# Mamba in four segments of 512 columns, with the projections of one segment beside the scans of another

## The reference

```python
def _mamba(x, in_w, conv_w, conv_b, xproj_w, dt_w, dt_b, A_log, D, out_w):
    xz = jnp.einsum('bld,ed->ble', x, in_w)
    xi, z = jnp.split(xz, 2, axis=-1)               # 512 channels each
    xi = jax.nn.silu(_dw_conv(xi, conv_w, conv_b))   # 4 taps along the tokens
    xdb = jnp.einsum('bld,ed->ble', xi, xproj_w)     # 128 + 16 + 16 rows
    dtr, Bm, Cm = (xdb[..., :DTR], xdb[..., DTR:DTR + DS], xdb[..., DTR + DS:])
    dt = jax.nn.softplus(jnp.einsum('blr,dr->bld', dtr, dt_w) + dt_b)
    y = _selective_scan(xi, dt, Bm, Cm, -jnp.exp(A_log), D)
    y = y * jax.nn.silu(z)
    return jnp.einsum('bld,ed->ble', y, out_w)
# scan, for each of 16 states: h = exp(dt * A) * h + (dt * x) * B;  y += h * C;  then y += x * D
h = gelu(img_patches @ w_in.T + b_in)
r = _mamba(h, fm...) + flip(_mamba(flip(h, 1), bm...), 1) + h
```

## Time and profile before

| | |
|---|---|
| median of 3 runs | 1244.85 us (1243.49 to 1244.88) |
| profiled execution | 1242.37 us, span of its trace 1240.3 us, mean granted TensorE clock 0.906 |
| lead-in of the Mamba, to the first scan | 543.0 to 625.0 us |
| scan, forward | 625.0 to 834.5 us |
| between the scans | 834.5 to 916.4 us |
| scan, backward | 916.4 to 1123.5 us |
| after the last product | 1123.5 to 1141.5 us |

### The profile page before, as it was taken

The page is one execution under the profiler, slowest core; times in us unless marked ns, Lnnn a source line. Parts: engine busy times, 40 slices in busy tenths (PEclk is TensorE's granted clock), DMA queues, the critical chain, the costliest instruction groups (busy, mean ns, idle before and its releaser), DMA issues. The chain is left out here.

```text
span 1240.3 us, 11914 instructions
## 1 busy us (share of the span) xinstructions
PE 990.9 (80%) x3880; PEld 620.1 (50%) x3880; DVE 914.3 (74%) x872; ACT 494.2 (40%) x804; POOL 689.1 (56%) x325
## 2 busy tenths in 40 slices
PE   6889858999999999959657676779947677668498
PEld 3566646888888888735312222226312222223376
DVE  4577746777777777755598999895399899994732
ACT  2666522434443344335733334343543333332231
POOL 1355522566655666500279999970069999991100
PEclk9899968999999999979877999889968888988799
DMA  3000024343244324120225444540314443530001
GB/s 102 1 1 0 1 85 138 105 132 118 89 118 119 122 85 118 47 72 1 106 102 167 138 169 170 168 141 1 106 35 168 169 168 138 173 132 0 1 1 34
DMA packets 42050, 115.92 MB, mean 93 GB/s; under 512 B 8752, under 2 KB 13872, under 8 KB 41888
## 3 DMA queue, kind: packets, MB, share of 16 engines
q1 hardware_dynamic: 42016, 115.50, 28.8%
HBM read 113.98 MB, written 1.51 MB: 93 GB/s over the span
## 5 line engine op out<-in xcount | busy, mean ns | idle before, releaser
L1143 POOL TENSOR_TENSOR uB<-u,Bb 128x1024 f32<-128x1024 f32 x128 | 304.1, 2398 | 34.2 <-DMA Cb<-bc_rows 13.6
L1224 PE MATMUL m_ps<-hV,ident 128*128 128x512 f32 x336 | 206.2, 750 | 129.0 <-DVE hV L1204 129.0
L768 POOL TENSOR_TENSOR lutw<-lutw,lt 128x860 f32<-128x860 f32 x80 | 200.1, 2501 | 149.0 <-DVE lt L745 143.3
L1199 DVE TENSOR_TENSOR_SCAN m_ps<-m_ps,uB 128x1024 f32<-128x1024 f32 x84 | 191.9, 2284 | 16.2 <-POOL uB L1143 15.7
L1224 PEld LDWEIGHTS m_ps<-hV,ident 128*128 128x128 f32 x336 | 67.8, 223 | 259.2 <-DVE hV L1204 205.9
L1166 ACT ACTIVATE m_ps<-zero 128x4 f32<-128x4 f32 x128 | 22.6, 177 | 269.2 <-DVE hV L1204 222.3
L1204 DVE TENSOR_TENSOR hV<-m_ps,Cb 128x1024 f32<-128x1024 f32 x84 | 102.9, 1225 | 9.0 <-DVE m_ps L1199 0.9
L1150 POOL TENSOR_TENSOR hP<-hS,Cb 128x1024 f32<-128x1024 f32 x44 | 103.8, 2358 | 6.2 <-DVE hS L1195 6.2
L1195 DVE TENSOR_TENSOR_SCAN hS<-m_ps,uB 128x1024 f32<-128x1024 f32 x44 | 100.3, 2280 | 1.1 <-POOL uB L1143 1.1
L1224 PE MATMUL m_ps<-hP,ident 128*128 128x512 f32 x176 | 90.5, 640 | 0.6 <-POOL hP L1150 0.6
L385 POOL TENSOR_TENSOR prob<-prob,ri 128x1024 f32<-128x1024 f32 x32 | 60.6, 1895 | 53.1 <-DVE ri L463 53.1
(11 more groups left out here) (223 smaller groups left out, 2035.3 us busy)
## 6 DMA issues: line engine op xcount, KB each, us to landing
Bb<-bc_rows SPq DMA_DIRECT2D x64, 512.0 KB, 3.5
Cb<-bc_rows SPq DMA_DIRECT2D x64, 512.0 KB, 4.9
wr<-in_moe_w SPq DMA_DIRECT2D x41, 384.0 KB, 4.2
cwb<-cw_rows SPq DMA_DIRECT2D x16, 512.0 KB, 4.0
cwb<-cw_rows SPq DMA_DIRECT2D x16, 384.0 KB, 4.5
cwb<-cw_rows SPq DMA_DIRECT2D x16, 256.0 KB, 3.8
lut_f<-in_lut_idx SPq DMA_DIRECT2D x1, 2144.0 KB, 8.7
cwb<-cw_rows SPq DMA_DIRECT2D x16, 128.0 KB, 3.9
```

Source lines behind the costliest of these rows:

```text
L768: e.tensor_tensor(part, part, lt[:, q, :], ALU.add).then_inc(s_la, 1)
L1143: e.tensor_tensor(uB[:, n % UBUF, :], u[:, d, :], Bb[:, q, :], ALU.mult).then_inc(s_ub, 1)
L1199: e.tensor_tensor_scan(a[:, way], a[:, way], uB[:, n % UBUF, way], 0.0, ALU.mult, ALU.add).then_inc(s_sc, 1)
L1224: mm = e.matmul(ya[n % 2][:, h * HALF:(h + 1) * HALF], g.ident[:, :], at[:, h * HALF:(h + 1) * HALF], start=False, stop=False, skip_group_ ...
```

## The change

The two directions are cut into four segments: seg 0 and 1 are the forward direction over the first and the second two sequences, seg 2 and 3 the backward one. One block holds all of it. A step now works on 512 columns (HALF), so there are 256 steps (STEPS), 64 for each segment (SSTEP) and 32 for each pair of channel blocks (PSTEP). `on_pool`, LATE and the numbers of uB, hV and hP buffers are as before; da has three banks instead of two. A row of B and of C is 256 KB each.

Only the projection of segment 0 stands ahead of the scans. Each engine has a `Side` program for each segment, a generator that names the step at which its next piece is due; after the engine's own work of a step, `advance` runs the pieces that are due. During segment s it does the projection of segment s + 1 (x and convolution in steps 2 to 26, B, C and low rank from 34, dt from 43), the gate's z of that segment, and the output projection of segment s - 1. What is left at the end of a segment is run by `finish`.

The convolution is four float32 matmuls with diagonal matrices for each channel block on PE; POOL makes the 16 diagonals (`tensor_scalar` of the unit matrix) of a direction, those of the backward direction in steps 36 to 51 of segment 0. ACT copies its result from PSUM and adds the bias; Silu of x and of z are one operation of 128 x 2048 each. Softplus keeps dt in PSUM (ln, addition and product with x), and ACT copies it to SBUF. The product hV of step n is now made after the scan of step n + 1. The store of B and C is issued by ACT. SP loads the backward direction's input weights after row 22 and those of x-projection and dt after row 32; ACT and DVE split the former at the end of segment 1. Eight PSUM banks: two sums ya, three da, three side banks.

```diff
+NSEG = 4
+NHS = HALF // SEQ
+PSTEP = 2 * DS
+SSTEP = 2 * PSTEP
+STEPS = NSEG * SSTEP
+ROWS = 3
+UBUF, CBUF, PBUF, DABUF = 3, 3, 2, 3
+LATE = 2
+GATE_AT = 2
...
+class Side:
+    def __init__(self, program):
+        self.program, self.due = program, -1
+    def advance(self, step):
+        while self.due <= step:
+            self.due = next(self.program, NEVER)
+    def finish(self):
+        self.advance(NEVER - 1)
...
+def place(n):
+    pair = n // PSTEP
+    return n // SSTEP, pair, 2 * (pair % 2) + n % 2, n % 2, n // 2, n // 2 % ROWS
...
+        ya = [c.ps(ctx, f"ya{i}", [P, HALF]) for i in range(2)]
+        da = [c.ps(ctx, f"da{i}", [P, HALF]) for i in range(DABUF)]
+        S0, S1, S2 = (c.ps(ctx, f"side{i}", [P, HALF]) for i in range(3))
+        DTB = [S2, S0, S1, S2]
...
+        def x_tensor(e, k, m):
+            if m:
+                e.wait_ge(s_raw, DB * k + m)
+            elif k:
+                e.wait_ge(s_u, DB * (k - 1) + 2)
+                e.wait_ge(s_dtc, DB * (k - 1) + 2)
+                e.wait_ge(s_zc, DB * k - 1)
+            yield from in_rows(e, k, m, S0, s_x)
+        def conv_tensor(e, k, m):
+            e.wait_ge(s_raw, DB * k + m + 1)
+            if m:
+                e.wait_ge(s_cv, DB * k + m)
+            elif k:
+                e.wait_ge(s_u, DB * (k - 1) + 3)
+                e.wait_ge(s_dtc, DB * (k - 1) + 3)
+                e.wait_ge(s_zc, DB * k)
+            for t in range(DCONV):
+                if t:
+                    yield
+                o = t if k < 2 else 2 * PADC - t
+                mm = e.matmul(S1[:, :], sc.dg[:, m, t, :], raw[:, m % 2, :, o:o + SEQ], start=t == 0,
+                              stop=t == DCONV - 1)
+            mm.then_inc(s_c, 1)
...
+            step = 2
+            for work in (x_tensor(e, k, 0), x_tensor(e, k, 1), conv_tensor(e, k, 0), x_tensor(e, k, 2),
+                         conv_tensor(e, k, 1), x_tensor(e, k, 3), conv_tensor(e, k, 2), conv_tensor(e, k, 3)):
+                for _ in work:
+                    step += 1
+                    yield step
+                step += 1
+                yield step
...
+        def side_tensor(e, seg):
+            if seg == NSEG - 1:
+                yield 26
+                yield from out_tensor(e, seg - 1, 26)
+                return
+            k = seg + 1
+            yield 2
+            yield from project_tensor(e, k)
+            yield 26
+            if k == 1:
+                yield from gate_tensor(e, k, [26, 28, 30, 32])
+            else:
+                yield from out_tensor(e, k - 2, 26)
+            yield 34
+            yield from rows_tensor(e, k)
+            yield 43
+            dt_tensor(e, k, 0)
+            yield 44
+            dt_tensor(e, k, 1)
+            yield 45
+            dt_tensor(e, k, 2)
+            yield 50
+            dt_tensor(e, k, 3)
+            if k > 1:
+                yield 51
+                yield from gate_tensor(e, k, [51, 54, 56, 58])
...
+        def exp_abs(e, k, d):
+            e.wait_ge(s_dm, DB * k + d + 1)
+            e.activation(e1[:, d % 2, :], DTB[d][:, :], ACT.Abs, bias=ws[k // 2].dtb[:, d:d + 1]).then_inc(s_ab, 1)
+            e.wait_ge(s_ab, DB * k + d + 1)
+            e.activation(e1[:, d % 2, :], e1[:, d % 2, :], ACT.Exp, scale=-1.0).then_inc(s_e1, 1)
+        def log(e, k, d):
+            e.wait_ge(s_mx, DB * k + d + 1)
+            e.wait_ge(s_e1, DB * k + d + 1)
+            e.activation(DTB[d][:, :], e1[:, d % 2, :], ACT.Ln, bias=1.0).then_inc(s_ln, 1)
+        def keep_dt(e, k, d):
+            e.wait_ge(s_u, DB * k + d + 1)
+            e.activation(dt[:, k % 2, d, :], DTB[d][:, :], ACT.Copy).then_inc(s_dtc, 1)
...
+        def side_scalar(e, seg):
+            if seg < NSEG - 1:
+                yield from project_scalar(e, seg + 1)
+            if seg == 0:
+                yield 32
+                copy_z(e, 1, 0)
+                yield 33
+                copy_z(e, 1, 1)
+            else:
+                yield 31
+                silu_z(e, seg)
+            if seg < NSEG - 1:
+                silu_x(e, seg + 1)
+            e.preload_act_table_set("natural_log_exp_and_others")
...
+        def softplus(e, k, d):
+            e.wait_ge(s_ln, DB * k + d + 1)
+            e.wait_ge(s_mx, DB * k + d + 1)
+            e.tensor_tensor(DTB[d][:, :], DTB[d][:, :], u[:, k % 2, d, :], ALU.add).then_inc(s_dt, 1)
+            e.wait_ge(s_dt, DB * k + d + 1)
+            e.tensor_tensor(u[:, k % 2, d, :], DTB[d][:, :], xi[:, k % 2, d, :], ALU.mult).then_inc(s_u, 1)
...
+                for r in range(STEPS // 2):
+                    q, s, seg = r % ROWS, r % DS, r // (SSTEP // 2)
+                    if r % (SSTEP // 2) == 0:
+                        e.wait_ge(s_bc, 16 * (seg + 1))
+                    if r >= ROWS:
+                        done = 2 * (r - ROWS) + 2
+                        e.wait_ge(s_ub, done)
+                        e.wait_ge(s_hv, vector_steps(done))
+                        e.wait_ge(s_hp, pool_steps(done))
+                    for i in range(2):
+                        e.dma_start(BC[:, q, i, :], dram["bc"][i * DS + s:i * DS + s + 1, half_of(seg)]
+                                    .broadcast_to([P, HALF])).then_inc(s_row[q], 16)
+                    if r == SSTEP // 2 - 10:
+                        e.wait_ge(s_z, 2 * DB)
+                        in_weights(c, dram, "bm", sc)
+                    if r == SSTEP // 2:
+                        e.wait_ge(s_dm, 2 * DB)
+                        e.wait_ge(s_xl, 2)
+                        dt_weights(c, dram, "bm", sc)
...
+                for n in range(STEPS + LATE):
+                    if n < STEPS:
+                        seg, pair, d, b, r, q = place(n)
+                        if n % PSTEP < 2:
+                            e.wait_ge(s_u, DB * seg + d + 1)
+                        if b == 0:
+                            e.wait_ge(s_row[q], 32 * (r // ROWS + 1))
+                        if n >= UBUF:
+                            e.wait_ge(s_sc, n - UBUF + 1)
+                        e.tensor_tensor(uB[:, n % UBUF, :], u[:, seg % 2, d, :], BC[:, q, 0, :],
+                                        ALU.mult).then_inc(s_ub, 1)
+                    m = n - LATE
+                    if m >= 0 and on_pool(m):
+                        k, q = pool_steps(m), place(m)[5]
+                        e.wait_ge(s_sc, m + 1)
+                        if k >= PBUF:
+                            e.wait_ge(s_ap, k - PBUF + 1)
+                        e.tensor_tensor(hP[:, k % PBUF, :], hS[:, k % 2, :], BC[:, q, 1, :],
+                                        ALU.mult).then_inc(s_hp, 1)
+                    side.advance(n)
...
+                def product(n):
+                    k, q = vector_steps(n), place(n)[5]
+                    if k >= CBUF:
+                        e.wait_ge(s_av, k - CBUF + 1)
+                    e.wait_ge(s_sc, n + 1)
+                    e.tensor_tensor(hV[:, k % CBUF, :], da[n % DABUF][:, :], BC[:, q, 1, :], ALU.mult).then_inc(s_hv, 1)
...
+                    e.wait_ge(s_da, 2 * n + 2)
+                    e.wait_ge(s_ub, n + 1)
+                    way = slice(None) if seg < 2 else slice(None, None, -1)
+                    a = da[n % DABUF]
+                    if on_pool(n):
+                        k = pool_steps(n)
+                        if k >= 2:
+                            e.wait_ge(s_hp, k - 1)
+                        e.tensor_tensor_scan(hS[:, k % 2, way], a[:, way], uB[:, n % UBUF, way], 0.0,
+                                             ALU.mult, ALU.add).then_inc(s_sc, 1)
+                    else:
+                        e.tensor_tensor_scan(a[:, way], a[:, way], uB[:, n % UBUF, way], 0.0,
+                                             ALU.mult, ALU.add).then_inc(s_sc, 1)
+                    if n and not on_pool(n - 1):
+                        product(n - 1)
+                    side.advance(n % SSTEP)
...
+                def add(n, at, done):
+                    return e.matmul(ya[n % 2][:, :], g.ident[:, :], at, start=False, stop=False,
+                                    skip_group_check=True).then_inc(done, 1)
```

More of the change, by code:

```diff
@@ L853, in split_weights @@
-def split_weights(c, name, sc):
-    s_wh, s_wl = c.sem(name + "_wh"), c.sem(name + "_wl")
-    parts = [slice(i * D, (i + 1) * D) for i in range(2 * DI // D)]
-    def high(e, w):
-        e.wait_ge(w.ready, w.count)
-        for p in parts:
-            e.activation(sc.wh[:, :, p], w.win[:, :, p], ACT.Copy).then_inc(s_wh, 1)
-    def low(e, w):
-        for i, p in enumerate(parts):
-            e.wait_ge(s_wh, i + 1)
-            e.tensor_tensor(sc.wl[:, :, p], w.win[:, :, p], sc.wh[:, :, p].bitcast(F32),
-                            ALU.subtract).then_inc(s_wl, 1)
-    return high, low
+NSEG = 4
@@ new lines, with on_pool @@
+NHS = HALF // SEQ
[6 more added lines that the diff above has]
+GATE_AT = 2
+NEVER = 10 ** 6
```

(52 more changed lines are left out.)

762 lines of the change are left out of this document (405 added, 357 removed).

## The result

The changed kernel takes 1286.8 us (median of 4 runs, 1283.44 to 1288.01), the kernel before, on the same chip, 1244.48 (4 runs): a ratio of 1.0337, with a 95% interval of 1.0316 to 1.0357. It is 42 us slower, where 1237 was predicted and 1262 was the upper end. The profiled execution took 1283.44, its span is 1281.7 us against 1240.3.

A forecast was written before the change was run, and what follows sets the result against it. In the scans, nine POOL operations plus the row-load latency L set the pace; 182 us had no scan. Lead-in 66, loop 513.5 and end 11 gave 590.5 against 598.5, -8.0, so 1237 us, range 1212 to 1262.

The forecast's parts named there:

- The lead-in: Stretch before the first scan, now projecting one segment of 512 columns: 66 us instead of 82, -16.
- The end: Stretch after the scans, two gates and eight matmuls of 0.87: 11 us instead of 18, -7.
- L: Time from release of a row buffer of B and C to the uB using its next row: 3.7 us, before 5.5.
- the page's fit: Skill page's DMA fit, 2.0 us plus bytes at 436 GB/s: 3.2 for the new pair, loop some 10 us shorter.
- The ring: Pace of the scan loop through the row buffers: nine POOL operations plus L, 9 x 1.22 + 3.7 = 14.7 us for eight steps.
- The bare loop: Scan loop before side work is added: 57.6 us for a pair of channel blocks, eight pairs 461.
- The side work: Additions to the loop where projections, gates and other work beside the scans don't fit: 52.5 us, making it 513.5.
- The weight split: Splitting the backward direction's input weights on DVE and ACT, placed beside segment 1: +4 us.
- (1): Rival: row loads keep nearly their latency; at L = 4.4 the loop takes 22 us more, 1259. Chance 0.18.
- (2): Rival: row loads keep up, POOL's or PE's work sets the loop's pace; 28 us less, 1209. Chance 0.14.
- (3): Rival: PE takes over in the loop at a clock below 0.945; 23 us more, 1260. Chance 0.12.
- (4): Rival: side work is pushed to segment ends, some 20 us each; +60, 1297. Chance 0.04.

The follow-up runs named there:

- the bare kernels: The changed kernel with all side work left out, every segment scanning the first's data: 1260.7 us with three row buffers, 1157.5 us with four.

## Why the prediction was wrong

By its own steps:

- **The lead-in**: 66 us predicted, 67.2 measured. Right, and so are its inner marks: PE starts on the projection at 556.4 (556.5 predicted) and ends the convolution at 580.9 (579.5).
- **The end**: 11 predicted, 13.6 measured (the last product ends at 1168.9, acc is complete at 1182.5). The eight matmuls took 3.7 us for each four, 3.5 costed; what was missing is the 3.1 us ahead of the first gate in which PE still works off its queued additions.
- **Durations of 512 columns**: uB every 1.22 to 1.24, a scan every 1.14, a product every 0.59. Right within 0.01 to 0.02.
- **L**: this is the step that failed first. 3.7 was taken, from "1.8 for 512 KB and 1.7 fixed": the second load of a pair lands 1.8 after the first, and I took that for the time of its bytes and halved it. It goes mostly with its 128 pieces, which the change doesn't halve. Measured: 4.74 in the first round, 4.88 in the median and up to 5.9 later, above even my bound of 4.4. The estimate of 10 us less by the page's fit holds only with 0.2 for release and wake-up added to its 3.2; without it, 32 x 0.5 is 16.
- **The ring**: this failed too. The step counted "nine POOL operations plus L", one ring with one L, as the kernel before had it. Beside it the change makes a second one, by the line of which I wrote that "Delaying the product by one scan removes the wait on the scan's own end": the delayed product of step 5 releases a row, and stands behind a scan that itself waits for one. It takes 6.9 + 2 L against 11.1 + L; at L = 4.2 they are equal, above that the second is the longer. At the 3.7 of the forecast it would have been the shorter one (14.3 against 14.8), so this step failed only together with the first. I had costed what the delay removes and not what it puts off.
- **The bare loop**: 461 predicted, 533.3 measured. With both corrections the sum holds: a round of 17.0, a pair of 4 x 17.0 - 1.2 = 66.8, eight pairs 534. The size of L alone, 4.9 for 3.7 in one ring, is 32 x 1.2 = 38 of the 72; the rest came with the second ring, of which the kernel with the product put back regains 17.6. The same formula gives 58.0 for a pair with half the pieces (11.1 + 3.7), where the first pair shows 58.1, and a round of 16.5 with one transfer of 256 pieces (6.9 + 2 x 4.8), where its first pair shows 16.5 to 16.7.
- **The side work**: 52.5 predicted, 5 of it for gates, start and end, which the bare kernels hold too. Against the other 47.5 it is 65.5 where the rows are in time, so its parts were sized too low by a quarter, and 25.4 in the changed kernel. The two terms were not independent, and adding them was an error in the other direction, of 22 to 27 us.
- **The weight split**, 4 us of the side work, was placed in the wrong segment, in the prediction and ahead of it: the trace has it in the last steps of segment 0 (741.5 to 753.7 us), where its cover is the same kind of steps. Nothing in the sum hangs on that.
- **Sum**: 67.2 + 533.3 + 25.4 + 13.6 = 639.5 against 598.5, +41.0; the spans differ by 41.4.

Of the rivals, **(1)** had the mechanism: the rows keep nearly their latency, and the kernel is slower. Its price was too small, 22 us, since it ended at L = 4.4 and counted L once in a round; at 4.9 and with two of them it is 72 on the loop. I had the rows that spoke for it, 32 KB in 1.7 us and 128 KB in 1.9, and gave more weight to the step from 3.5 to 4.9 within a pair, which no row split into bytes and pieces. **(2)**, the rows keep up, is what the kernels with four buffers or the early B load show, not this one. **(3)**: the granted clock in the loop was 0.89, under the 0.945 from which PE was to take over, yet PE waited for hV and not the other way round (105.8 us, 88 times). Its per-step load was taken as if a step lasted 1.84; it lasts 2.2. **(4)** is refuted: side work at the segments' ends costs 141 us, and the changed kernel has nothing of the kind.

The signs named beforehand did their work. "A POOL idle of about 1.3 once in eight steps" became 2.5 and a second stop, and "an L outside 3.2 to 4.2" is what would make the prediction wrong, and did.

## What to carry to other kernels

When a change halves the tiles, list what doesn't halve: the latency from the release of a buffer to the use of its next load went from 5.5 to 4.9 us only, while the lead of a given number of buffers, counted in time, is halved. Follow every ring of releases through the new order of instructions, above all behind an operation that is put off by a step, and count how often the latency stands in each; here one deferred product put it there twice. And look at what a buffer's release waits for: a half that was read early can be loaded again early, which here was worth as much as a whole further buffer (1224.6 us either way, 19 under the kernel before).

## What the runs showed of the hardware that was not expected

- The latency of a row broadcast to 128 partitions follows its bytes little: 128 pieces of 4 KB are used 3.80 us after the release of their buffer (median), 256 pieces of 2 KB after 4.88 to 4.90, whether they are one transfer or two; 256 pieces of 128 bytes still take 4.34. A load of 256 pieces from as many places in DRAM landed in 2.8, so this is shown for broadcast rows alone.
- With 128-byte pieces the landing depends on which row is read (2.3 us for states 12 to 15, 2.7 for the others, first load of two); with 2 KB pieces it doesn't. Why is open.
- Spread over time the same loads land sooner: the median from issue to landing is 3.3 us with the early B load and 4.1 in the changed kernel, for the same 256 transfers of 256 KB. There the B load of a row and its C load wait for different things and no longer always go out together.

```profile
BC<-bc_rows SPq DMA_DIRECT2D x256, 256.0 KB, 3.3
```
